# Attention block on one core: where a slot's value products stand in TensorE's order

## What is computed

```python
mod = (silu(c) @ wmod)                         # sa, ca, ga, sb, cb, gb
h = layernorm(x) * (1 + ca) + sa
q, k, v = split(h @ w_qkv)                     # 16 heads of 8 channels
attn = softmax(q @ k.T / sqrt(128))            # 512 x 512 for each head
x = x + ga * ((attn @ v) @ w_out)
h = layernorm(x) * (1 + cb) + sb
x = x + gb * moe(h)                            # 8 experts, top 2 of a softmax router
```

## Time and profile before

| | |
|---|---|
| median of 3 runs | 659.65 us (657.90 to 661.47) |
| the profiled execution's own time | 658.46 us |
| its span in the trace | 656.6 us |
| PE, DVE, ACT, POOL busy | 89%, 80%, 66%, 46% of the span |
| attention stage, by the trace | about 50 to 441 us |
| mean granted clock of TensorE | 0.971; 1.00 from 60 us to the end of the stage |

### The profile page before, as it was taken

The page is one execution under the profiler, slowest core; times in us unless marked ns, Lnnn a source line. Parts: engine busy times, 40 slices in busy tenths (PEclk is TensorE's granted clock), DMA queues, the critical chain, the costliest instruction groups (busy, mean ns, idle before and its releaser), DMA issues.

```text
span 656.6 us, 10230 instructions
## 1 busy us (share of the span) xinstructions
PE 582.8 (89%) x3349; PEld 272.0 (41%) x3349; DVE 526.5 (80%) x769; ACT 433.0 (66%) x823; POOL 299.6 (46%) x426
## 2 busy tenths in 40 slices
PE   4259899999999999999999998788799999999995
PEld 2202222322322322322322322226677777777773
DVE  3597888888888888888888898527888888888884
ACT  1206877787887887787787788784555555555552
POOL 4434205315315315315315213435586786776763
PEclk9757999999999999999999999999999999999998
DMA  7712703403403403503403401263244444445401
GB/s 186 173 66 49 225 3 88 142 19 75 156 19 85 146 19 75 156 19 83 148 18 81 151 18 35 60 175 131 81 142 148 130 143 147 130 143 145 138 23 33
DMA packets 49092, 65.76 MB, mean 100 GB/s; under 512 B 9544, under 2 KB 30544, under 8 KB 49040
## 3 DMA queue, kind: packets, MB, share of 16 engines
q1 hardware_dynamic: 46416, 64.32, 33.7%
q10 hardware_dynamic: 2624, 0.79, 0.5%
HBM read 47.26 MB, written 17.83 MB: 99 GB/s over the span
## 4 chain that ended last, share of the span: by engine, by line
PE 44%; DVE 17%; ACT 15%; POOL 14%; issue 6%; DMA 2%; SPq 1%; ACTq 1%; POOLq 0%; DVEq 0%
PE o_acc L1230 19%; POOL hid_lo L624 11%; PE ring L1216 9%; ACT probs L668 9%; PE s_row L1203 8%; DVE probs L1073 8%; DVE negmax L871 6%; ACT hid_hi L808 3%; POOL h_lo L630 2%; PE ring L1130 1%; PE s_row L1157 1%; PE ring L1135 1%; DVE probs L1063 1%; PE ring L1132 1%; SPq L308 1%
## 5 line engine op out<-in xcount | busy, mean ns | idle before, releaser
L871 DVE TENSOR_REDUCE negmax<-s_row 128x2 f32<-128x1024 f32 x256 | 306.0, 1220 | 57.6 <-PE s_row L1203 57.0
L668 ACT ACTIVATE probs<-ring 128x512 f32<-128x512 f32 x512 | 273.4, 600 | 79.7 <-PE ring L1216 78.2
L624 POOL TENSOR_TENSOR hid_lo<-probs,hid_hi 128x512 fp32r<-128x512 f32 x87 | 128.5, 1493 | 62.9 <-ACT hid_hi L808 62.9
L1216 PE MATMUL ring<-q_stack,k_stack 64*128 64x512 bf16 x512 | 129.3, 382 | 19.7 <-ACT probs L668 17.4
L1230 PE MATMUL o_acc<-probs,v_aug 128*32 128x512 f32 x1024 | 136.5, 605 | 0.0
L1203 PE MATMUL s_row<-k_stack,q_stack 64*128 64x512 bf16 x512 | 103.5, 402 | 27.6 <-DVE negmax L871 15.4
L808 ACT ACTIVATE hid_hi<-probs 128x512 fp32r<-128x512 f32 x88 | 55.6, 632 | 85.3 <-DVE probs L1073 85.3
L1203 PEld LDWEIGHTS s_row<-k_stack,q_stack 64*128 64x128 bf16 x512 | 24.7, 93 | 146.0 <-DVE negmax L871 66.8
L511 POOL CAST negmax_parts<-negmax 128x16 bf16<-128x16 f32 x32 | 6.3, 196 | 158.3 <-DVE negmax L871 158.3
L1073 DVE TENSOR_TENSOR probs<-probs,q_stack 128x512 f32<-128x512 f32 x56 | 61.9, 1105 | 15.4 <-POOL hid_lo L624 14.2
L1216 PEld LDWEIGHTS ring<-q_stack,k_stack 64*128 64x128 bf16 x512 | 35.0, 94 | 71.2 <-ACT probs L668 61.0
(11 more groups left out here) (155 smaller groups left out, 681.6 us busy)
## 6 DMA issues: line engine op xcount, KB each, us to landing
q_scr<-q_parts SPq DMA_DIRECT2D x48, 128.0 KB, 2.4
k_scr<-k_parts SPq DMA_DIRECT2D x48, 128.0 KB, 2.4
q_stack<-q_scr SPq DMA_DIRECT2D x8, 768.0 KB, 6.2
k_stack<-k_scr SPq DMA_DIRECT2D x8, 768.0 KB, 7.6
q_stack<-combT_scr SPq DMA_DIRECT2D x24, 256.0 KB, 3.4
k_stack<-combT_scr SPq DMA_DIRECT2D x16, 224.0 KB, 3.0
q_stack<-combT_scr SPq DMA_DIRECT2D x16, 192.0 KB, 2.8
q_stack<-combT_scr SPq DMA_DIRECT2D x16, 160.0 KB, 2.6
```

The source lines that it names most:

```text
L624: nc.gpsimd.tensor_tensor(hid_lo[k % HIDDEN][:], weighed[(par + k) % 2], hid_hi[k % HIDDEN][:], ALU.subtract).then_inc(s["hid_split"], 1)
L668: nc.scalar.activation(probs[t % 2][:, j, :], ring[COL_PLACE[b, t, j] % RING][:], ACT.Exp, scale=INV_SCALE).then_inc(s["exp_done"], 1)
L871: nc.vector.tensor_reduce(negmax[n % 2][:, 2 * half:2 * half + 2, qc], s_row[ROW_PLACE[b, t, half] % 2][:], AX.X, ALU.max, negate=True).th ...
L1216: nc.tensor.matmul(ring[place % RING][:], k_stack[par][at:at + KS, head // 2, P * kc:P * (kc + 1)], q_stack[par][at:at + KS, head // 2, :] ...
```

## The change

In each slot the value products of slot t - 1 are issued after R1 and before C2 and C3, and not behind C3 and its task. Nothing else is changed: the same instructions, ring places and buffers, and the order on ACT and DVE is the same. The waits in front of the value products are issued with them.

```diff
                             row_scores(b + 1, 1 - par, t + AHEAD - SLOTS, half)
+                        if half == 1 and t > 0:
+                            weigh(b, par, t - 1)
+                        elif half == 1 and not first:
+                            weigh(b - 1, 1 - par, SLOTS - 1)
                         for j in range(2 * half, 2 * half + 2):
                             col_scores(b, par, t, j)
                         turn((t, half))
-                    if t > 0:
-                        weigh(b, par, t - 1)
-                    elif not first:
-                        weigh(b - 1, 1 - par, SLOTS - 1)
                     turn((t, 2))
```

## The result

| | before | changed |
|---|---|---|
| median of the runs | 660.56 us (657.90 to 661.99) | 697.55 us (695.24 to 701.99) |
| span of the profiled execution | 656.6 us | 693.4 us |
| from one start of q to the next, batches 1 to 5 | 49.3 us (49.27 to 49.55) | 54.58 us |

The changed kernel is slower by 5.8%: the ratio is 1.058, 95% interval 1.055 to 1.062. 696 us was forecast. Of the four runs of the changed kernel the one with the profile is the fastest, 695.24 us; its span is 36.8 us longer than the one before.

The account below looks back on a forecast made before the run. It took a PE and ACT loop to bound slots without a task, and PE's issue the slot with v. Batches 1 to 5 +26.5, batch 6 +4.9, first +3.4, last +2.3: together +37, 696 us, own range 687 to 706.

Parts of the forecast that it names:

- the sum: Full batch, slots 0 to 15, added from distances between starts: 54.6 us against 49.3 before, +5.3 a batch.
- The plain slot: Slot without a task: one column product's wait for an exp goes, another's comes, as long; change 0.
- The wait of W itself: Value products' wait for the previous slot's last exp costs nothing; the third column product waited for the same exp before.
- The first batch: First batch +3.4 us: q, k, v (about 0.7, 0.8, 0.9), xT twice (0.7), small losses around the maxima (0.3).
- The last two: Batch 6 +4.9 us, as it lacks xT (0.37); the last batch +2.3 us.
- The expert stage: Head and expert stage: no change, save 0.3 us for the last column product before the stage's end, left out.
- The clock: Attention stage: clock stays at 1.00, 2.4 GHz; PE's new waits are at most 0.8 us long.
- a rival: Clock falls to 1.2 GHz for a tenth of the attention stage: 37 us more, to 733; 3 in 100.
- faster: Third exp done when the next slot's second column product comes; covered exp waits are gain: 30 us, to 629; 3 in 100.
- e2: Slot without a task: exp of the previous slot's third column product; starts at 0.20, frees its bank at 0.85 us.
- half the loss: Task slots: PE's waits partly overlap hidden ones, or another rhythm arises; half lost: +18, to 677; 8 in 100.
- no effect: All slots, with tasks too, only exchange one wait for another, if DVE sets their length: about 660; 2 in 100.

Follow-up runs that it names:

- kernel with halves in chosen slots but not in the last batch: Against the kernel before: value products in two halves of 256 columns in slots 0, 5, 7, 12 to 15, not in the last batch; 651.03 us.
- the kernel that has the halves there, too: Against the kernel before: value products in two halves of 256 columns in slots 0, 5, 7, 12 to 15, last batch included; 648.31 us.

## Why the prediction was right

*Slot by slot.* Time from one R0 to the next in the changed kernel, slot 3 from 219.36 on, slots 0 and 1 from the batch that follows, against the sum (us):

| slot | 0 | 1 | 2 | 3 | 4 | 5 | 6 | 7 | 8 | 9 | 10 | 11 | 12 | 13 | 14 | 15 |
|---|---|---|---|---|---|---|---|---|---|---|---|---|---|---|---|---|
| forecast | 2.86 | 3.98 | 3.93 | 3.28 | 3.63 | 3.51 | 3.79 | 2.60 | 4.23 | 2.94 | 3.46 | 3.79 | 2.86 | 2.83 | 3.46 | 3.46 |
| measured | 2.87 | 3.99 | 3.94 | 3.30 | 3.56 | 3.52 | 3.80 | 2.61 | 4.23 | 3.01 | 3.47 | 3.70 | 2.87 | 2.83 | 3.47 | 3.41 |

A full batch is 54.6 against 54.58. Small misses: the router's eight products take 0.99 us to the next start and not the 1.10 of v; combT takes 0.54 and not 0.59; in slot 4 the 0.09 us that I gave to DVE's lateness behind o0 did not come; in slot 9 W starts 0.07 later behind the copy of `o_acc`. The prediction also had PE's busy time at about 46 of 54 us; it counts as 49.70. The sum went by starts and did not use it.

*The plain slot* exchanged one wait for another of the same length, as worked out. *The wait of W itself* cost nothing: in slot 7 W starts 1.38 us behind R0, as in the sum, where it follows from PE's own order. *DVE* stayed a follower: PE waits less for it than before.

*The first batch.* Forecast +3.4; the interval between its q and the next went from 46.88 to 48.56 us, +1.7, and q itself starts 0.1 later. q was at the lower clock in the kernel before and not here, which gave back about a microsecond. The prediction had no term for that:

```profile
55.01 2.07 PE L1130 MATMUL ring<-hT,wqk_sb 128*128 128x512 f32 x2
```

```profile
55.10 1.12 PE L1130 MATMUL ring<-hT,wqk_sb 128*128 128x512 f32 x2
```

The first is of the kernel before, the second of the changed one.

*The last two.* Forecast +7.2 together; from the last q to the first expert product it went from 92.5 to 100.9 us, +8.4. So the total is nearer than its parts: 1.7 too much in the first batch and 1.2 too little in the last two nearly cancel, which is luck. The five full batches carry the rest, +26.2 against +26.5. *The expert stage* is as long as it was: 215.5 us from its first product to the end of the span, and 215.9.

*The clock.* The prediction kept it at 2.4 GHz in the whole stage, and from 60 us into the last batch that held. It failed for 4 us in the last batch, in slot 10 (columns as in the earlier trace rows):

```profile
454.00:459.00 5.00, 3.42 (x21) 0.81 (x17) 0.69 (x1) 3.59 (x8) 4.21 (x11) 1.00 0.50 147
459.00:463.00 4.00, 3.05 (x14) 1.05 (x15) 1.61 (x2) 1.08 (x2) 1.04 (x2) 0.60 0.06 20
```

There the transposition x1T and W took 1.02 and 1.86 us to the next start, instead of 0.59 and 1.00: 1.3 us, about what the last batches have over the forecast. The clock fell after two longer idle times of PE, 1.06 us ahead of the transposition of maxima and 1.27 us until x1n was there; that these brought it down is not shown (see the last section).

By the Trainium skill (TensorE: Matmul & The Clock Gate, section on PSUM-queue depth-cycling) short idles between groups of matmuls, from cycling through PSUM banks, can make the clock swing; I had weighed that as a rival. The full batches of this case do not bear it out: 27 waits for a bank in a batch, at most 0.8 us long, left the clock at 1.00.

The three other rivals fell as they stood. For "faster": in slot 7 C1 waits for e2 (the two would have been 0.44 us apart where 1.07 are needed). For "half the loss": slot 8 lost the whole 0.90 us. For "no effect": the task slots with v, q and k lost 0.90, 0.70 and 0.81 us, and it was slot 7, without a task, that exchanged one wait for another as long.

## What to carry to other kernels

In this ring of three banks, with four products to a slot, the gap between the second pair of products and the next had to be filled just as the one between the first and the second; a long job is worth most in the gap that has no other. Before moving a block on the busiest engine, go through the ring place by place: for whose evacuation (the copy or exp that empties a bank) does the next writer wait, when did that product start, and how much work stands between. Where one block must cover two gaps, cut it along the dimension that shortens its pieces, and only in the slots where a wait is to be had for it.

## What was not expected of the hardware

The clock at its lower level in the last batch is not told by the place of the value products. The kernel with halves in chosen slots but not in the last batch has the last batch of the kernel before, and yet shows it; the kernel that has the halves there, too, doesn't; the kernel before doesn't either. First the one without halves in the last batch, then the one with them (columns as in the earlier trace rows):

```profile
410.00:420.00 10.00, 8.09 (x41) 2.12 (x33) 2.30 (x3) 5.38 (x12) 6.33 (x10) 0.75 0.44 135
420.00:426.00 6.00, 5.74 (x26) 2.20 (x30) 0.56 (x3) 3.42 (x8) 1.09 (x1) 0.56 1.01 252
```

```profile
410.00:420.00 10.00, 7.39 (x47) 1.99 (x43) 3.08 (x8) 7.10 (x15) 6.71 (x12) 1.00 0.28 80
420.00:426.00 6.00, 5.90 (x52) 2.27 (x52) 1.17 (x9) 5.19 (x11) 3.55 (x4) 1.00 0.94 281
```

The length of an idle time doesn't tell it either. Here are PE's two longest idle times ahead of the stretch in the last batch, first in the kernel before, where the clock stayed at 1.00, then in the kernel with halves in chosen slots:

```profile
417.75 0.39 PE L1216 MATMUL ring<-q_stack,k_stack 64*128 64x512 bf16 x1 [0.96 <-ACT probs L668]
425.94 0.63 PE L1161 MATMUL ring<-ident,x1n 128*128 128x128 f32 x4 [0.93 <-POOL x1n L473]
```

```profile
406.91 0.39 PE L1216 MATMUL ring<-q_stack,k_stack 64*128 64x512 bf16 x1 [0.96 <-ACT probs L668]
415.11 1.09 PE L1161 MATMUL ring<-ident,x1n 128*128 128x128 f32 x4 [0.94 <-POOL x1n L473]
```

The same instructions wait equally long, and only in the second are the four transpositions slow, 1.09 us and not 0.63. From there to the start of the third W it is 10.45 us in the second, 6.50 in the kernel before: 3.95 us for the clock. Behind the last q the two kernels with halves in chosen slots differ by 5.2 us in their profiled executions (94.88 and 89.64 to the first expert product). So most of that is the clock and about 1.3 us the order; how it is in the other executions, and so in the medians of 651.03 and 648.31 us, isn't known. What decides whether the clock falls there, and whether it does so in every execution of a kernel, stays open.
